# A recurrent attention network on one core: the attention score's last product moved from TensorE matmuls to a transposing row sum on VectorE

## What is computed

```python
hs = _gru(hist, gru_W, gru_U, gru_b)
emb = jnp.concatenate([hs, news_b - hs, news_b, hs * news_b], axis=-1)
a = jax.nn.relu(jnp.einsum('bti,ij->btj', emb, att_W1) + att_b1)
a = jax.nn.relu(jnp.einsum('bti,ij->btj', a, att_W2) + att_b2)
ats = jax.nn.sigmoid(jnp.einsum('bti,ij->btj', a, att_W3) + att_b3)
def au_step(h, xs):
    u = jax.nn.sigmoid(xu_t + h @ au_Uu)
    r = jax.nn.sigmoid(xr_t + h @ au_Ur)
    c = jnp.tanh(xc_t + r * (h @ au_Uc))
    u_ = at_t * u
    hn = (1.0 - u_) * h + u_ * c
```

## Time and profile before

| | |
|---|---|
| median of three runs | 1932.87 us (1932.86 to 1934.15) |
| span of the profiled execution, first to last instruction | 1930.2 us |
| PE busy | 1914.1 us, 99% of the span |
| POOL busy | 1639.8 us, 85% |
| DVE busy | 1501.7 us, 78% |
| ACT busy | 1458.1 us, 76% |
[...]

### The profile page before, as it was taken

One profiled execution on the slowest core, in us unless ns is written; L12 is line 12 of the kernel. 1 busy time (PEld: TensorE's weight loads), 2 busy tenths in 40 slices (PEclk: granted clock), 3 DMA queues, 4 the chain that ended last, 5 costly groups with the idle time before them and its releaser, 6 DMA issues.

```text
span 1930.2 us, 46212 instructions
## 1 busy us (share of the span) xinstructions
PE 1914.1 (99%) x17555; PEld 998.4 (52%) x17555; DVE 1501.7 (78%) x2349; ACT 1458.1 (76%) x2470; POOL 1639.8 (85%) x1395
## 2 busy tenths in 40 slices
PE   8999999999999999999999999999999999999998
PEld 4455555555555555555555555555555555555554
DVE  7887777777777777777777777777777777777787
ACT  7877777777777777777777777777777777777775
POOL 7788888888888888888888888888888888888874
PEclk9999999999999999999999999999999999999999
DMA  3121111112111211121121112111211211121110
GB/s 126 55 72 51 50 61 61 50 50 72 52 54 50 72 50 50 53 69 50 50 72 50 53 53 71 51 50 50 72 50 50 70 52 50 53 70 54 40 45 23
DMA packets 37854, 110.20 MB, mean 57 GB/s; under 512 B 4348, under 2 KB 4732, under 8 KB 31304
## 3 DMA queue, kind: packets, MB, share of 16 engines
q1 hardware_dynamic: 37560, 107.57, 17.4%
q10 hardware_dynamic: 144, 0.26, 0.1%
HBM read 107.39 MB, written 0.42 MB: 56 GB/s over the span
## 4 chain that ended last, share of the span: by engine, by line
PE 93%; ACT 2%; DVE 2%; POOL 1%; issue 1%; DMA 0%; SPq 0%; DVEq 0%; ACTq 0%; POOLq 0%
PE ps L1128 87%; PE ps L1211 3%; PE ps L1129 1%; PE ps L1202 1%; POOL hn L326 0%; POOL x_lo L345 0%; ACT x_hi L501 0%; ACT ps L549 0%; ACT a_hi L486 0%; DMA x<-in_xs 0%; DVE ps L828 0%; PE ps L1414 0%; ACT ps L594 0%; PE ps L1415 0%; DVE ps L810 0%
## 5 line engine op out<-in xcount | busy, mean ns | idle before, releaser
L1128 PE MATMUL ps<-h_hi,w_hi 128*64 128x512 f16 x1384 | 524.9, 379 | 6.0 <-DVE a_lo L816 1.5
L1129 PE MATMUL ps<-h_hi,w_hi 128*64 128x512 f16 x1384 | 524.9, 379 | 0.0
L1129 PE MATMUL ps<-h_lo,w_hi 128*64 128x512 f16 x1384 | 524.5, 379 | 0.0
L1129 PE MATMUL ps<-h_hi,w_lo 128*64 128x512 f16 x1384 | 524.5, 379 | 0.0
L1128 PE MATMUL ps<-h_lo,w_hi 128*64 128x512 f16 x1384 | 524.5, 379 | 0.0
L1128 PE MATMUL ps<-h_hi,w_lo 128*64 128x512 f16 x1384 | 524.5, 379 | 0.0
L332 POOL TENSOR_TENSOR hn_lo<-hn,hn_hi 128x512 f16<-128x512 f32 x200 | 232.6, 1163 | 159.8 <-ACT hn_hi L481 159.7
L326 POOL TENSOR_TENSOR hn<-h,news 128x512 f32<-128x512 f32 x200 | 256.1, 1281 | 77.5 <-DVE h L1001 77.5
L627 ACT ACTIVATE ps<-gt,p_rest 128x512 f32<-128x512 f32 x185 | 127.7, 690 | 201.8 <-DVE gt L998 201.8
L345 POOL TENSOR_TENSOR x_lo<-x,x_hi 128x512 f16<-128x512 f32 x196 | 227.5, 1161 | 17.7 <-ACT x_hi L501 13.5
L405 POOL TENSOR_TENSOR d<-h,hc 128x512 f32<-128x512 f32 x186 | 237.6, 1278 | 0.0
(11 more groups left out here) (171 smaller groups left out, 6817.6 us busy)
## 6 DMA issues: line engine op xcount, KB each, us to landing
x<-in_xs SPq DMA_DIRECT2D x199, 256.0 KB, 3.0
score<-score_rows SPq DMA_DIRECT2D x48, 1024.0 KB, 4.7
news<-in_xs SPq DMA_DIRECT2D x4, 256.0 KB, 5.1
x<-score_rows SPq DMA_DIRECT2D x1, 1024.0 KB, 4.2
h<-score_rows SPq DMA_DIRECT2D x1, 1024.0 KB, 4.2
score_rows<-s_rows SPq DMA_DIRECT2D x50, 8.0 KB
p_rest<-in_pack_rest SPq DMA_DIRECT2D x1, 776.0 KB, 7.8
p_att<-in_pack_att SPq DMA_DIRECT2D x1, 290.0 KB, 4.8
```

What stands on the lines that cost most here:

```text
L1128: m.matmul(ps[0:H, bank, :], weights[:, 0:H], moving, start=start, stop=stop)
L1129: return m.matmul(ps[H:P, bank, :], weights[:, H:P], moving, start=start, stop=stop)
```

## The change

PE no longer forms the score. `scores`, `w3_pair`, `high_2` and `low_2` go. `relu_2` now writes an f32 tile a2 in SBUF and frees the PSUM bank (`a2_ready` instead of `a2lo_ready`). DVE multiplies a2 in place by the sign of w3, a column per partition, and sums over partitions: `tensor_reduce` with `apply_transpose`, which sums 32 partitions of each quarter and takes the 512 elements in a pattern of 32 blocks with a step of 16 elements, so that 128 x 512 becomes 128 x 16 (`sum_2`). The two quarters that belong to one item are added later: SP lifts the upper 32 partitions of each half down by DMA (`lift_partials`), DVE adds 128 x 32 (`total_of`), ACT takes the sigmoid of 128 x 32 (`scores_of`), and SP stores with two DMAs and broadcasts as before. The tile score has three buffers instead of one (and the late copies in x32 and h32 go). The sum stands where the low parts stood, in slots with low % 4 == 2; `total_of` stands ahead of all else on DVE in slots with low % 4 == 0, `scores_of` on ACT in the same slot between the high part of hn and the gate gu.

```diff
+    FOLDED = TILED + 3
...
+    def folds_of(low):
+        return low % NC == FOLDED % NC and has(low - FOLDED)
...
+            def lift_partials(done):
+
+                sp.wait_ge(part_ready, done)
+                for k in range(2):
+                    sp.dma_start(part_up[k * H:k * H + Q, :, :], part[k * H + Q:(k + 1) * H, :, :]).then_inc(part_landed, 16)
+
+            def spread_scores(group, buffer):
+
+                if not isinstance(group, int) or group > 0:
+                    sp.wait_ge(score_landed, 16 * group)
+                sp.wait_ge(s_ready, NC * group + NC)
+                rows = score_rows.rearrange("(g k) (b j) -> k b g j", k=2, b=Q)
+                for k in range(2):
+                    sp.dma_start(rows[k], s_col[k * H:k * H + Q, :, :]).then_inc(rows_stored, 16)
...
+            def scores_between(step, c, buffer):
+                known = isinstance(step, int)
+                if c == 0 and (not known or step >= 3):
+                    spread_scores(step - 3, buffer)
+                if c == 2 and (not known or step >= 2):
+                    lift_partials(NC * step - NC)
...
             def relu_2(p, count):
 
                 act.wait_ge(a2_pe[p], count)
-                a.activation(ps[:, B_PAIR[p], :], ps[:, B_PAIR[p], :], ACT.Relu, bias=b_att2[:, 0:1],
-                             scale=w3_col[:, 3:4]).then_inc(a2p_ready[p], NC)
-
-            def high_2(p, count):
-
-                act.wait_ge(a2p_ready[p], count)
-                a.activation(a2_hi[:, p, :], ps[:, B_PAIR[p], :], ACT.Copy).then_inc(a2hi_ready[p], NC)
...
+                if not isinstance(count, int) or count > NC:
+                    act.wait_ge(part_ready, count - NC)
+                a.activation(a2[:, p, :], ps[:, B_PAIR[p], :], ACT.Relu, bias=b_att2[:, 0:1],
+                             scale=w3_col[:, 3:4]).then_inc(a2_ready[p], NC)
+
+            def scores_of(count):
+
+                act.wait_ge(total_ready, count)
...
+                a.activation(s_col[:, :, :], total[:, :, :], ACT.Sigmoid, bias=p_att[:, PACK_ATT["b3"]]).then_inc(s_ready, NC)
...
-            def low_2(p, count):
-
-                dve.wait_ge(a2hi_ready[p], count)
-                v.tensor_tensor(a2_lo[:, p, :], ps[:, B_PAIR[p], :], a2_hi[:, p, :], ALU.subtract).then_inc(a2lo_ready[p], NC)
+            def sum_2(p, count):
+
+                dve.wait_ge(a2_ready[p], count)
+                v.tensor_scalar(a2[:, p, :], a2[:, p, :], w3_col[:, 2:3], None, ALU.mult).then_inc(a2s_ready[p], NC)
+                dve.wait_ge(a2s_ready[p], count)
+                v.tensor_reduce(part[:, p, :], a2[:, p, :].rearrange("p (b j) -> p j b", b=Q), AX.X, ALU.add,
+                                apply_transpose=True).then_inc(part_ready, NC // 2)
+
+            def total_of(count):
+
+                dve.wait_ge(part_landed, 8 * count)
...
+                v.tensor_tensor(total[:, :, :], part[:, :, :], part_up[:, :, :], ALU.add).then_inc(total_ready, NC)
...
-            def scores(count, bank=B_SCORE):
-
-                for p in range(2):
-                    pe.wait_ge(a2lo_ready[p], count)
-                for part in (a2_hi, a2_lo):
-                    for p in range(2):
-                        done = m.matmul(ps[p * H:(p + 1) * H, bank, :], w3_pair[:, :], part[:, p, :],
-                                        start=part is a2_hi, stop=part is a2_lo)
-                done.then_inc(score_pe, NC)
...
@@ slot on PE @@
-                    if score_of(low - 1):
-                        pe.wait_ge(s_ready, scored(s0 + (off - 1)))
...
-                        pe.wait_ge(a2lo_ready[0], paired(s0 + (off - 1)))
+                        pe.wait_ge(a2_ready[0], paired(s0 + (off - 1)))
...
-                if score_of(low):
-                    if gated:
-                        pe.wait_ge(gr_ready, late(LAG))
-                    elif gru:
-                        pe.wait_ge(r_ready, at(0))
-                    scores(scored(s0 + off))
```

More of the change, by code:

```diff
@@ L96, in rec_kernel @@
     SPLIT_X, SPLIT_G = LAG - 3, LAG + 1
-    assert (LOOP_HI - LOOP_LO) % HIST == 0
+    STEP_LO, STEP_HI = 6, 6 + (T - 6) // 3 * 3
+    assert (LOOP_HI - LOOP_LO) % HIST == 0 and HIST == 3 * NC
     def has(item):
@@ L107, in paired, with folded @@
         return n - (TILED - NC)
[L109 to L118, removed]
+    def folds_of(low):
+        return low % NC == FOLDED % NC and has(low - FOLDED)
+    def folded(n):
+        return n - (FOLDED - NC)
     def gxh_bank(item):
@@ L284, in _, with whole_step @@
             sp.dma_start(p_rest[:, :], pack_rest).then_inc(rest_landed, 16)
[L285 to L291, removed]
+            def whole_step(step, buffer):
                 for c in range(NC):
                     load_step(step, c)
[L294 to L308, removed]
+                    scores_between(step, c, buffer)
+            for step in range(2, STEP_LO):
+                whole_step(step, step % 3)
+            with sp.Fori(STEP_LO, STEP_HI, 3) as step:
+                for k in range(3):
+                    whole_step(step + k, k)
+            for step in range(STEP_HI, T):
+                whole_step(step, step % 3)
+            for step in range(T, T + 3):
+                scores_between(step, 0, step % 3)
+                if step < T + 2:
+                    scores_between(step, 2, None)
             sp.wait_ge(y_ready, 1)
@@ L366, in early, with gated_share @@
                     state_news_low(low - 1, low)
-            def gated_share(item, count, landed, rows=score):
+            def gated_share(item, count, landed):
                 pool.wait_ge(gu_ready, count)
                 pool.wait_ge(score_landed, landed)
-                g.tensor_tensor(gus[:, item % 2, :], gu[:, item % 2, :], rows[:, item % NC, :], ALU.mult).then_inc(gus_ready, 1)
+                g.tensor_tensor(gus[:, item % 2, :], gu[:, item % 2, :], score[:, item % HIST // NC, item % NC, :], ALU.mult).then_inc(gus_ready, 1)
             pool.wait_ge(xlo_ready, LOW_DVE)
@@ L431, in late @@
                     pool.wait_ge(ge_ready, item - 2)
-                gated_share(item - 1, item, 16 * ((item - 1) // NC + 1), score if item <= ITEMS - 2 * NC else late_scores[(item - 1) // NC - T + 2])
+                gated_share(item - 1, item, 16 * ((item - 1) // NC + 1))
                 if low == ITEMS:
@@ L639, in slot @@
                     state_news_high(low - 1, at(1))
+                if folds_of(low):
+                    scores_of(folded(s0 + off))
                 if has(low - LAG):
```

129 lines of the change are left out of this document (51 added, 78 removed).

## The result

The changed kernel takes 1920.58 us (median of 4 runs, 1918.98 to 1920.78) against 1932.86 (4 runs, 1931.91 to 1934.15): ratio 0.9934, interval 0.9922 to 0.9947. It is faster, as forecast, but by 12.3 us and not by 20.0, and 0.6 us outside the range. The profiled execution took 1920.78 us, its span is 1918.6 (before 1930.2).

What follows compares the result with a forecast made beforehand. TensorE's gapless matmul stream was taken to bound the kernel; 19.4 us from the middle plus 0.6 from the ends off the 1930.2 span gives 1910.2, plus 2.67 to the median, 1912.9 us. Range 1909.5 to 1920.

Steps and rivals of the forecast that it cites:

- The pass is what binds: Gapless middle: removing four score matmuls, 0.43 us of TensorE's stream, at each of 45 places saves 19.4 us.
- likeliest case: Whole run: TensorE stays gapless in the middle, period falls from 37.99 to 37.55 us; time 1912.9, own range 1909.8 to 1917.5.
- The multiplication: On DVE, SBUF to SBUF: 0.42 us, bounds 0.29 and 0.69, plus up to 1.28 us waiting for POOL.
- The transposing sum: On DVE, in no profile row: 0.69 us as one pass, up to 1.38 us as two.
- the rule: In the middle: with a sum of R us, over about 0.9, t is 2R - 1.4 us late against PE.
- The slack of 1.6 us: Behind t in the middle: up to 1.6 us of lateness costs nothing before PE waits for g or h.
- The race for SBUF: DVE's first multiplication against POOL's hn: POOL waits for the end of h, so DVE comes first and hn slips 0.3 us.
- rival 2: POOL's hn starts before the first multiplication: 1962 us with sums of 1.38, partly 1918 to 1930; 5% slower, 4% partly.
- Queues at nothing: SP's two lifts and one more store per group cost nothing; a lift has over 12 us until needed.
- The ends: Head and tail: TensorE passes gain 1.7 us, ACT's copies 1.5, DVE waiting behind POOL -2.5; net +0.6, between -4.5 and +3.
- Rival 1: Sum over about 1.5 us makes PE wait, deciding from 1.71; three passes, 2.07 us, give 1965 us, slower; 6%.
- rival 3: The pass does not bind: another engine's period or a wait in the next slot absorbs the gain, 1930 to 1933; 4%.

Runs made afterwards that it cites:

- no_sign: Changed kernel with the multiplication by the sign left out: 1912.38 us, ratio to the kernel before 0.9892.
- sign_psum: Changed kernel with ScalarE rectifying in PSUM and VectorE's multiplication reading PSUM and writing SBUF: 1919.68 us, ratio to the kernel before 0.9928.
- contig: Changed kernel with the transposing sum reading 32 consecutive elements instead of elements 64 bytes apart, output order left wrong: 1915.81 us, ratio to the kernel before 0.9909.
- no_total: Changed kernel without the addition of the lifted half, the sigmoid taking the lower half's sums alone: 1918.72 us, ratio to the kernel before 0.9922.
- the last two runs: Changed kernel with rectifier writing in order for contiguous sums, sign by ScalarE, addition one slot up; second also has later sign passes and sums: 1913.15 and 1914.39 us.
- perm_sign_late_fold: sign_late_fold plus ScalarE's rectifier writing the tile in the order in which the sum reads 32 consecutive elements: 1914.39 us, ratio to the kernel before 0.9902.
- sign_late_fold: Changed kernel with sign by ScalarE's second pass, addition and sigmoid one slot up, sign passes and sums one or two instructions later: 1913.19 us, ratio 0.9897.

## Why the prediction was right in direction and wrong in size

1. **The pass is what binds, 45 places x 0.43 = 19.4 us:** right, 19.43. The whole middle, the "likeliest case", was right: no gap on TensorE, a period of 37.555 us.
2. **The multiplication, 0.42 us, the second one longer behind GpSimd:** 0.47 to 0.48 where it runs freely. In the middle the second one did not wait either: it began at 1001.52, when GpSimd's gus (1000.37 to 1001.64) was all but over. In the ends they took up to 1.46.
3. **The transposing sum, 0.69 to 1.38 us:** 1.058. Lateness of t 0.9 us, where the rule gave 0.72. The slack of 1.6 us behind it was tested by the doubled sums and stands, to some 0.1 us.
4. **The race for SBUF:** VectorE came first, 998.78 against hn's start at 998.95, and hn took 1.46 us there where it had 1.28; rival 2 did not occur.
5. **Queues at nothing:** right in the middle, which has no wait. In the ends GpSimd waited 0.8 us in all for a score and VectorE never for a lift, so nothing of the loss was found there.
6. **The ends, net +0.6, between -4.5 and +3: this step failed.** They lost 7.8 us. I priced there what VectorE would *wait* for GpSimd, -2.5, and put what it would *work* at nothing, although the same sentence says that VectorE is on the path. The account from the traces: in the ends the new instructions last 4.85 + 3.67 us (head and tail; ten multiplications), 6.36 + 4.23 (ten sums) and 2.68 + 1.31 (five additions), 23.1 in all. At 0.47 us for a multiplication alone and 0.18 for an addition, 6.9 of that is waiting for GpSimd and 16.2 is work; ten subtractions of 0.69 us go, so VectorE works 9.3 us more. Against it stand 5.9 us in which VectorE had waited for ScalarE's copy ahead of those ten subtractions, 0.17 to 1.49 us each; the longest and the shortest in VectorE's timeline of the kernel before:

```profile
94.13 0.69 DVE L805 TENSOR_TENSOR a_lo<-ps,a_hi 128x512 f16<-128x512 f32 x1 [1.49 <-ACT a_hi L555]
...
1843.34 0.69 DVE L805 TENSOR_TENSOR a_lo<-ps,a_hi 128x512 f16<-128x512 f32 x1 [0.17 <-ACT a_hi L555]
```

The passes of TensorE, put at 1.7, no run here measures. 9.3 + 6.9 - 5.9 - 1.7 = 8.6, near the 7.8 measured. So the work, put at nothing, is the term that failed. Two others were mis-sized, the waits at 6.9 in place of 2.5 and the copies at 5.9 in place of 1.5; that they cancel is luck. The runs show that such time is paid on the chain, working or waiting: 8.44 us for 8.52 us of multiplications (no_sign), 1.09 for 1.12 (sign_psum), 4.45 for 4.67 us of shorter sums and multiplications (contig), and 1.9 to 3.5 for 4.0 us of additions (no_total).

Rival 1 needed R over 1.71 to lose and was at 1.06; rival 3 did not occur. None of the rivals was about the ends, so the range had no case that held 1920.6.

What stays open: how the 7.8 us divide between the parts, since prices on one chain don't add once another engine takes over, as the last two runs show; and why perm_sign_late_fold is no faster than sign_late_fold, as the longer waits for ScalarE account for 3 of the 3.5 us but not for the rest.

## What to carry to other kernels

A stage without a gap on one engine and the ramps at both ends have different bounds; cost each instruction once per stage, and in a ramp where the receiving engine goes from one instruction to the next, count the moved work at its full length, waits on top. An edit that is free in the steady state can lose 40% of its gain in two ramps that are a tenth of the run. Look at the order in which a reduction reads its elements before the choice of engine: here the same numbers in another order, arranged by an engine whose pass did not get longer by it (0.768 us in both orders), were worth more than a third of what the whole change brought.

## What the runs showed of the hardware

- A transposing sum of 128x512 f32 to 128x16 takes 0.712 us when it reads 32 neighbours at a time, hardly more than an elementwise pass of VectorE (0.69), and 1.058 us when they stand 64 bytes apart. ScalarE reading PSUM with the same step showed none of it, 0.768 us in both orders.
- A multiplication by a column of scalars on 128x512 f32 takes 0.47 to 0.48 us from SBUF to SBUF when GpSimd rests, up to 1.46 us when it works, and 0.72 to 0.75 us from PSUM, whether GpSimd works or not. An addition of 128x32 takes 0.18 us or, behind GpSimd, 1.25.
